# Folding the layer-norm modulation into the weights, turning x by DMA, and a ring of four PSUM banks

## What is computed

```
mod = silu(c) @ wmod                      # c: 2 x 512, wmod: 512 x 3072
sa, ca, ga, sb, cb, gb = six parts of mod, each 512 wide, one row per batch
h = layernorm(x) * (1 + ca) + sa
q, k, v = split(conv3(h) + conv_b)        # 3 taps, 512 -> 3 x 128, SAME padding
qh, kh, vh = projections to 16 heads of 64, each with a bias
o = softmax(causal(qh kh^T / 8)) vh       # in blocks of 128 tokens
x = x + clamp(ga) * ((o @ wo + bo) @ proj_w + proj_b)
h = layernorm(x) * (1 + cb) + sb
base = h @ base_w^T + base_b;  r = h @ A^T (64);  logits = h @ router^T (16)
combine = the two largest softmax weights of the logits, normalised
x = x + clamp(gb) * (base + 0.5 * (combine x r) @ B)
```

## Time and profile before

| what | value |
|---|---|
| time, median of 3 runs | 522.66 us (520.54 to 524.2) |
| the profiled execution | 522.22 us |
| its span, first to last instruction | 520.4 us |
| mean granted TensorE clock | 0.967 |
| TensorE matmul busy | 459.0 us, 88% |
| VectorE, ScalarE, GpSimd busy | 334.1, 302.9, 287.1 us |
| DMA | 53.32 MB moved, mean 102 GB/s |

### The profile page before, as it was taken

The page is one execution under the profiler, slowest core; times in us unless marked ns, Lnnn a source line. Parts: engine busy times, 40 slices in busy tenths (PEclk is TensorE's granted clock), DMA queues, the critical chain, the costliest instruction groups (busy, mean ns, idle before and its releaser), DMA issues.

```text
span 520.4 us, 10871 instructions
## 1 busy us (share of the span) xinstructions
PE 459.0 (88%) x4112; PEld 294.1 (57%) x4112; DVE 334.1 (64%) x597; ACT 302.9 (58%) x966; POOL 287.1 (55%) x320
## 2 busy tenths in 40 slices
PE   2949998999799999999999999999979999973756
PEld 0227664667577657856765757756645664532422
DVE  3486788899877776777775575575548677425110
ACT  1532755797687878775686636576548665512200
POOL 3264373271667363457656666856736796815811
PEclk9968999999899999999999999999999999997979
DMA  8992132732342424423262434354253464530141
GB/s 329 354 375 86 42 82 42 230 95 42 82 97 68 82 62 88 77 62 82 56 128 42 103 60 96 91 82 103 62 122 72 92 131 78 118 82 26 35 101 42
DMA packets 110292, 53.32 MB, mean 102 GB/s; under 512 B 100768, under 2 KB 100896, under 8 KB 109856
## 3 DMA queue, kind: packets, MB, share of 16 engines
q1 hardware_dynamic: 110096, 52.60, 40.9%
q10 hardware_dynamic: 144, 0.02, 0.1%
HBM read 23.25 MB, written 4.19 MB: 53 GB/s over the span
## 4 chain that ended last, share of the span: by engine, by line
PE 57%; DVE 12%; issue 8%; ACT 8%; POOL 7%; DMA 7%; SPq 1%; POOLq 0%; ACTq 0%; DVEq 0%
PE F L842 15%; PE C L924 14%; PE C L842 10%; PE S L964 3%; DMA xb<-in_x_dram 3%; PE WB L981 3%; ACT prob L589 3%; PE WB L842 3%; PE S L958 2%; PE F L892 2%; DVE p L768 2%; DMA gT<-g 2%; PE S L892 2%; PE T L1005 2%; DMA wma<-in_wmod_dram 2%
## 5 line engine op out<-in xcount | busy, mean ns | idle before, releaser
L924 PE MATMUL C<-hT,cw 128*128 128x256 f16 x864 | 106.5, 277 | 3.5 <-POOL hT L426 3.2
L924 PEld LDWEIGHTS C<-hT,cw 128*128 128x128 f16 x864 | 83.9, 99 | 22.7 <-POOL hT L426 4.7
L842 PE MATMUL F<-btw,gT 128*128 128x512 f16 x384 | 87.8, 386 | 9.8 <-DMA gT<-g 9.8
L589 ACT ACTIVATE prob<-S,nms 128x128 f32<-128x128 f32 x256 | 89.9, 378 | 7.6 <-DVE p L768 6.8
L473 POOL TENSOR_TENSOR prob<-prob,rinv 128x1024 f32<-128x1024 f32 x32 | 61.5, 1923 | 46.7 <-DVE rinv L773 46.6
L560 ACT ACTIVATE qk<-C,bqk 128x256 f16<-128x256 f32 x128 | 52.7, 480 | 31.6 <-PE C L842 31.3
L842 PEld LDWEIGHTS F<-btw,gT 128*128 128x128 f16 x384 | 37.6, 100 | 55.5 <-DMA gT<-g 11.6
L748 DVE SCALAR_TENSOR_TENSOR qk<-C,bqk,qk 128x256 f16<-128x256 f32 x128 | 54.7, 475 | 14.8 <-ACT qk L560 14.4
L842 PE MATMUL C<-cv,pw 128*128 128x256 f16 x384 | 52.8, 281 | 8.2 <-DVE xb L789 3.6
L589 ACT ACTIVATION_READ_ACCUMULATOR prob<-S,nms 128x1 f32 x256 | 55.6, 217 | 0.0
L768 DVE SCALAR_TENSOR_TENSOR p<-prob,p 128x1024 f16<-128x1024 f32 x32 | 46.5, 1452 | 6.5 <-ACT p L598 6.2
(11 more groups left out here) (140 smaller groups left out, 775.1 us busy)
## 6 DMA issues: line engine op xcount, KB each, us to landing
xa<-in_x_dram SPq DMA_DIRECT2D x8, 512.0 KB, 4.1
xb<-in_x_dram SPq DMA_DIRECT2D x8, 512.0 KB, 4.7
out_dram<-xb SPq DMA_DIRECT2D x16, 256.0 KB, 2.1
wmb<-in_wmod_dram SPq DMA_DIRECT2D x1, 3072.0 KB, 14.3
cw_raw<-in_cw_dram SPq DMA_DIRECT2D x3, 768.0 KB, 11.9
wma<-in_wmod_dram SPq DMA_DIRECT2D x1, 2048.0 KB, 8.7
bt_raw<-in_btw_dram SPq DMA_DIRECT2D x2, 1024.0 KB, 8.7
pw_raw<-in_pw_dram SPq DMA_DIRECT2D x3, 512.0 KB, 15.8
```

The costliest lines, as they stand in the source:

```text
L589: ins = nc.scalar.activation(prob[:, h], S[h // 4][:, (h % 4) * P:(h % 4 + 1) * P], ACT.Exp, bias=nms[:, i % 2, h:h + 1], scale=S_SCALE, a ...
L842: ins = nc.tensor.matmul(dst, stat(a), mov(b), start=first and i == 0, stop=last and i == 2)
L924: ins = nc.tensor.matmul(bank_c[:, 0:CH], cw[:, i, a, tap, c, :], hT[:, j % 2, b, c, tap:tap + CH], start=step == 0, stop=step == STEPS - 1)
```

## The change

Three things, and a schedule planned anew around them.

1. *Modulation in the weights.* Conv, base, router and A weights of a batch are multiplied by (1 + ca) or (1 + cb) per input channel when they are split; the shifts sa and sb become bias vectors (new stages `vb`, `fbias`, `lb`). As (1 + ca) differs between the batches, these weights are loaded again and split again for batch 1 (new `ra` loads, splits 11 to 16). `modT` is now computed directly in columns: `cols` is 32 fp32 matmuls with wmod as stationary operand (128 columns) and silu(c) moving (2 columns); `row` 0, 1, 3 and 4 are gone. At the edges of a batch the conv bias differs in one token column, which gets an instruction of its own.
2. *x turned by DMA.* The normalised x is split into fp16 first (ScalarE high, GpSimd low), then two DMA transposes of 128 x 1024 fp16 turn each chunk (stage `hs` for the first layer norm, `hs2` for the second). The TensorE transposes and the ScalarE modulation are gone, and so is GpSimd's cast. `lr` becomes a three-pass fp16 matmul from the same turned tile; its evacuation goes to VectorE with a bias.
3. *The T banks go to C*, which is a ring of four for `c`, `qk`, `v`, `pr` and `lr`.

The core of the diff:

```diff
-        T = [psum(f"T{i}") for i in range(2)]
-        C = [psum(f"C{i}") for i in range(2)]
+        C = [psum(f"C{i}") for i in range(4)]
...
@@ SyncE
-            sp.dma_start(xa[:, 0], xin[0]).then_inc(ld_xa[0], 16)
-            sp.dma_start(wma[:, :, 0:2, :], wmod_v[:, :, 0:2, :]).then_inc(ld["wma"], 16)
-            sp.dma_start(xa[:, 1], xin[1]).then_inc(ld_xa[1], 16)
-            for n in range(3):
-                sp.dma_start(cw_raw[:, n], cw_in[:, n]).then_inc(ld[f"cw{n}"], 16)
+            for i in range(2):
+                sp.dma_start(xa[:, i], xin[i]).then_inc(ld_xa[i], 16)
+            for c in range(DC):
+                sp.dma_start(wma[:, c, 0:2, :], wmod_v[:, c, 0:2, :]).then_inc(ld[f"wma{c}"], 16)
+            sp.dma_start(cw_raw[:, 0], cw_in[:, 0]).then_inc(ld["cw0"], 16)
...
+                if s == "hs":
+                    sp.wait_ge(h_lo, j + 1)
+                    if j >= 2:
+                        k, idx = bank(C_USE["c", j - 2, 2])
+                        sp.wait_ge(c_full[k], idx + 1)
+                        sp.wait_ge(h_ready, H_DONE[j - 1])
+                    for b in range(2):
+                        sp.dma_start_transpose(
+                            hT[:, j % 2, :, :, OWN + b * P:OWN + (b + 1) * P].rearrange("p m c q -> p (m c) q"),
+                            h16[:, b].rearrange("p m d -> p (m d)")).then_inc(h_moved, 16)
+                    if j == 1:
+                        for n in range(1, 3):
+                            sp.dma_start(cw_raw[:, n], cw_in[:, n]).then_inc(ld[f"cw{n}"], 16)
...
+                elif s == "hs2":
+                    sp.wait_ge(h2_lo, j + 1)
+                    if j > 0:
+                        sp.wait_ge(fb_read, 2 * j)
...
+                    for b in range(2):
+                        sp.dma_start_transpose(h2[:, :, :, b * P:(b + 1) * P].rearrange("p m c q -> p (m c) q"),
+                                               h216[:, b].rearrange("p m d -> p (m d)")).then_inc(h2_moved, 16)
...
@@ GpSimd
-                    nc.gpsimd.tensor_copy(hT[:, slot, HI, :, 1:CH + 1], hf[:]).then_inc(h_hi, 1)
-                    pool.wait_ge(h_hi, j + 1)
-                    nc.gpsimd.tensor_tensor(hT[:, slot, LO, :, 1:CH + 1], hf[:], hT[:, slot, HI, :, 1:CH + 1],
-                                            ALU.subtract).then_inc(h_ready, 1)
+                elif s == "hs":
+                    pool.wait_ge(h_hi, j + 1)
+                    nc.gpsimd.tensor_tensor(h16[:, :, LO], xa[:, j % 2], h16[:, :, HI], ALU.subtract).then_inc(h_lo, 1)
...
@@ ScalarE
-                    for g in range(2):
-                        k, idx = bank(T_USE["ln", j, 0] + g)
-                        act.wait_ge(t_full[k], idx + 1)
-                        for c in (2 * g, 2 * g + 1):
-                            ins = nc.scalar.activation(hf[:, c], T[k][:, (c % 2) * CH:(c % 2 + 1) * CH], ACT.Identity,
...
+                elif s == "hs":
+                    act.wait_ge(xn_ready, 2 * j + 2)
+                    if j > 0:
+                        act.wait_ge(h_moved, 32 * j)
+                    nc.scalar.activation(h16[:, :, HI], xa[:, j % 2], ACT.Copy).then_inc(h_hi, 1)
...
@@ TensorE
-                        for c in range(2):
-                            for b in range(2):
-                                ins = nc.tensor.transpose(T[k][:, c * CH + b * P:c * CH + (b + 1) * P],
-                                                          src[:, b, (2 * g + c) * P:(2 * g + c + 1) * P], ident[:])
...
+                            for k in range(DC):
+                                if m == c == 0:
+                                    pe.wait_ge(ld[f"wma{k}" if n == 0 else "wmb"], 16)
+                                ins = nc.tensor.matmul(m_bank(stage)[:, at:at + NB],
+                                                       (wma if n == 0 else wmb)[:, k, m, c * P:(c + 1) * P],
+                                                       silT[:, 0, k * NB:(k + 1) * NB], start=k == 0, stop=k == DC - 1)
...
+                elif s == "vb":
+                    pe.wait_ge(ld[f"cw{n}"], 16)
+                    pe.wait_ge(m_done, max(M_USE["cols", 0, 0] + 1, m_before(stage)))
+                    for tap in range(TAPS):
+                        for c in range(DC):
+                            ins = nc.tensor.matmul(m_bank(stage)[:, tap * NB:(tap + 1) * NB], cw_raw[:, n, c, tap, :],
+                                                   modT[:, 0, c, :], start=c == 0, stop=c == DC - 1)
...
-                    for b in range(2):
-                        for c in range(DC):
-                            ins = nc.tensor.matmul(T[k][:, b * ARW:(b + 1) * ARW], hf2[:, c, b * P:(b + 1) * P], arT[:, c, :],
-                                                   start=c == 0, stop=c == DC - 1)
-                    ins.then_inc(t_full[k], 1)
+                    for b in range(2):
+                        for c in range(DC):
+                            ins = passes(C[k][:, b * ARW:(b + 1) * ARW], lambda m: h2[:, m, c, b * P:(b + 1) * P],
+                                         lambda m: arw[:, m, c, :], c == 0, c == DC - 1)
+                    ins.then_inc(c_full[k], 1)
```

492 lines of the change are left out of this document (265 added, 227 removed).

## The result

The changed kernel takes 527.33 us (median of 20 runs, 523.31 to 531.52) against 521.33 us for the kernel before (20 runs, 519.34 to 524.2) on the same chips: ratio 1.0107, 95% interval 1.0088 to 1.0125. The forecast was 507 us, so it is 20 us off and has the wrong sign. In a later session the same kernel gave 525.78 us, ratio 1.0106 (1.0073 to 1.0139). Each ratio is taken over the executions within 1.5% of the fastest of their kernel. Its runs spread over 8 us and follow the clock: at a mean granted clock of 0.961 or more they take 523.3 to 525.6 us, at 0.949 or less 530.6 to 531.5.

The account below looks back on a forecast made before the run. TensorE was taken to bound the middle, with head and tail chains over several engines. Span 520.4 - 1.0 - 4.5 - 6 - 4 = 504.9, with 1.8 outside it 506.7, say 507 us; forecast case 499 to 514, range 496 to 525.

Parts of the forecast that it names:

- TensorE's work, -1.0: TensorE after the first convolution starts: removed and added matmul work nearly cancel, 1.0 us less; bounds -9 and +13.
- The head, -4.5: Before the first convolution: it starts at 32.9 us instead of 37.4, 4.5 us earlier; bounds 29 to 41.
- The ring and the middle, -6: Middle of the run: waits for banks and xn go, less new stalls, net 6 us less; bounds -16 and +5.
- 4 us of new stalls: Middle: charge for 14 pairs of DMA transposes holding SyncE's in-order queue, 4 us more.
- 10.2 us of waits that were to go: Middle: TensorE's waits on C for qk and pr (6.4 us) and for xn (3.8 us) were to vanish.
- SyncE's queue turns into the bound: Rival, chance 0.13: transpose pairs hold SyncE's queue; gain gone from about 1.1 us a pair, 538 us at 2.5.
- The tail, -4: Last chunk: earlier reload moves VectorE's add 4.7 us earlier, router loses 0.5; 4 us less, bounds -7 to +4.
- 2.3 of delay behind the store: Tail: the last probabilities' transpose stands behind chunk 5's store, so pv:7:3 starts some 2.3 us later.
- slow-turning rival: Rival, chance 0.02: in head and tail a transpose pair takes 12.8 us, not 4.4, giving 524 us.

Follow-up runs that it names:

- e1: Changed kernel with both sets of modulation columns made by row stages and small transposes, as in the kernel before; 524.49 us, ratio 1.0063 to the kernel before.
- e7: Changed kernel leaving out three quarters of the two-column sums (second modulation columns, second and third convolution offsets) behind the first convolution; 517.05 us, ratio 0.9923.
- e12: Changed kernel with the edits of e1 and e11 joined: columns by row and early turning of the last residual; 526.41 us, ratio 1.0088.
- e14: Changed kernel with convolution offsets from split fp16 weights and the second modulation columns by row; 527.11 us, ratio 1.0086.
- e15: Changed kernel with convolution offsets from split fp16 weights and both sets of modulation columns by row; 522.36 us, ratio 1.0018.
- e9: Changed kernel leaving out three quarters of the second and third convolutions' offset sums, modulation columns whole; 520.4 us, ratio 0.9989.
- e13: Changed kernel with convolution offsets computed from split fp16 weights, the first offset stage moved behind the first split; whole reference computed; 518.77 us, ratio 0.995.
- e4: Changed kernel with 4 KB DMAs in place of x's DMA transposes, from chunk 2 (convolutions) and chunk 1 (feed-forward); 518.63 us, ratio 0.9954.
- e8: Changed kernel with 4 KB DMAs in place of 14 DMA transposes, those for the feed-forward part alone; 522.92 us, ratio 1.0035.
- e3: Changed kernel with the last transpose of probabilities (ph:7:3) moved ahead of the store of chunk 5's second half; 529.56 us, ratio 1.0155.
- e11: Changed kernel with halving and turning of the last chunk's residual moved ahead of chunk 6's first-half addition and store; 527.28 us, ratio 1.0122.

## Why the prediction was wrong, step by step

**TensorE's work, -1.0: right in the sum at full clock, and blind to the clock.** From start to start `lr` takes 0.87 us for a group of 24 (449.01 to 449.88) and `vb` 1 takes 2.60 (39.12 to 41.72), both as forecast. `cols:1` was put at 6.9 and takes 9.51, because from 71.5 to 81.7 us the clock is at its lower level, 1.2 GHz. The sum took every duration at full clock and had no term for what the new stages do to it. The window from 60 to 90 us lost an estimated 6.8 us that way, as worked out above, and the runs' median clock is 0.955 instead of 0.967. The profiles point at the second columns: in all nine that have `cols:1` as 64 such records and the shared ring, a half-clock stretch begins between 70 and 76 us, 10.2 us long in six, 13.7 in two and 6.8 in one, and the five that have it shorter or by row (e1, e7, e12, e14, e15) hold only stretches of 3.4 us from 59 to 79 us; the kernel before has none there. The offsets have their part only by the medians: e9 and e13 have clocks of 0.9625 and 0.967 and fell by more than the time taken out, but their profiles keep the 10.2 us. That two-column matmuls as such do it is not shown: e13 has more of them.

**The head, -4.5: right in the start, and of little worth.** The convolution starts at 33.71 (forecast 32.9), 3.7 us earlier. `cols:0` ended at 24.3, not 22.5: 64 records at 216 ns, twice the 107 of the upper level, the slow end of the bounds. The pair of transposes landed and the halo was there by 33.7, 4.9 us after its issue (4.4 forecast for landing alone). The loads behind `hs:1`, issued from 31.46 on, were put at nothing. TensorE shows no wait for them, but VectorE stood 3.54 us for x of chunk 2 until 50.90. That is a second path to the end of chunk 0's convolution, no shorter than TensorE's own: taking out 4.1 us of offsets there (e9) moved this end by 0.1 us. From the start of the convolution to its last step for chunk 0 it took 30.5 us, where it had been 23.6, so the lead of 3.7 us was a delay of 3.2 by then. Part of this was forecast as added work (two offset stages, `row:2` and `pick`).

**The ring and the middle, -6: the first step that failed.** The removed waits were real and went (the rows on C and `xn`). The "4 us of new stalls" was the number that failed: e4 measures the turning behind the head at 8.7 us, e8 half of it for half the transposes. Of the 10.2 us of waits that were to go, the middle's idle time shows 0.8 (17.1 against 16.3). Part of the cost is `lr`'s wait for `h` (2.5 us less in e4, 4.1 less in e8), part is at `gT`, `pt` and the probabilities (6.1 us less together in e4, 4.0 in e8), which were there before and now share the queue and its order. How much of it falls in the middle isn't settled: by e8 little does, 0.8 us by the end of chunk 7's convolution. The median landing of `gT` rose from 4.4 to 5.0 us, the queue's share from 40.9% to 54.0%. The rival "SyncE's queue turns into the bound" had this mechanism, its size too high: 8.7 / 13 = 0.7 us a pair, where the rival put 2.5 and its turning point at 1.1. It took no more to lose, since the tail and the clock failed as well.

**The tail, -4: a wait moved.** The reload was issued at 455.55 and the bias was added at 460.43 instead of 466.75, as forecast. Next late, and not asked for, was `pr`: `pv:7:3` started 3.5 us later (2.3 forecast), `wo` ran 4.2 us instead of 2.8 in a stretch at the lower clock, and VectorE's add ended at 468.7, since it had to wait for `pr`, and not at 465.3 (470.0 before). `xn` was ready 1.3 us earlier, not 4.7. From there to the end of `lr` it took 12.2 us, above the 9 to 11 of the forecast, since GpSimd's subtraction stood behind the addition for chunk 6 and the transposes behind that of `gT` (issued at 480.65). Idle time behind 450 us, up to the last matmul at 515.9 and 517.7: 65.9 - 45.1 = 20.8 us before, 67.7 - 45.7 = 22.0 after. Both attempts to mend the order (e3, e11) moved the wait to another place of the same tail.

**The slow-turning rival** is settled: one transpose of x lands 3.3 us after its issue (median), and the pair of the tail, issued at 480.65, was there at 485.65, so 5.0 us and not 12.8. The Trainium skill ("VectorE: DVE Perf Modes", section "The three transpose paths") has 1309 ns for a 128x128 block by DMA; here 8 blocks land in 3.3 us, 0.41 us a block with the issue in it, so its price is too high for this kernel. Whether its advice to turn on TensorE where possible holds here no run shows: turning by DMA cost 8.7 us (e4), and the 14 groups of transposes that it replaced behind the head had been put at 12.2 us of TensorE's time.

**In one sum**, for the two profiled executions, where 522.3 - 504.9 = 17.4 us of span are to be accounted for:

- To the start of the convolution, 3.7 us gained instead of 4.5: 0.8.
- From there to `pv:7:3` it took 424.5 us against 417.3 (33.71 to 458.21, and 37.41 to 454.69). This is 7.2 more, where the forecast has 4.7 less (1.0 of work and 6 of waits gone, 2.3 of delay behind the store): 11.9. TensorE's idle time in this stretch grew by 1.0 us (20.25 in e11, 19.25 before) instead of falling by 3.7, and that is the stalls' term. The clock, which has no term in the forecast, makes about 6 us by an estimate: the listed half-clock stretches, at half their length, come to 10.2 us against 6.3, and the first 3.8 us of convolution ran at 213 ns a matmul.
- From `pv:7:3` to the end it took 64.1 us against 65.7, 1.6 less where the forecast has 6.3 less: 4.7, the tail.

So the new stalls and the delay of `pv:7:3` account for some 5 us, the clock for some 6, the tail for some 5; the rest is 0.8 of the head and 1.4 of work. The other 3 us of the 20 lie between this profile and the median of its kernel, as the profiled execution is faster than it. Beside that, e13 shows that 7.0 to 8.6 us could be had from another form of the offsets. The forecast put the second and third at 5.1 us, and they took 5.6 from start to start; that own time is not where the loss sits.
